# First attention: query and key parts placed by DMA through DRAM, one head to a half of the array's rows

## What is computed

```python
qkv = layernorm(x) @ w_qkv + b_qkv              # x: (16, 512, 256)
q, k, v = split into 16 heads of 16 columns
scores = einsum('bhqd,bhkd->bhqk', q, k) * 16 ** -0.5
# heads 0..3:  causal mask;  heads 4..15: causal and at most 64 tokens back
w = softmax(scores); ctx = w @ v
x = x + ctx @ w_out + b_out
```

## Time and profile before

| what | value |
|---|---|
| median of three runs | 3148.2 us (3143.63 to 3151.32) |
| span of the profiled execution, its own time | 3151.3 us, which is the slowest run (3151.32) |
| attention A within it | from the start to 1048.8 us, where SP issues the next phase's first load |
| share of the span busy: PE, DVE, ACT, POOL | 90%, 70%, 48%, 45% |

### The profile page before, as it was taken

One profiled execution on the slowest core, in us unless ns is written; L12 is line 12 of the kernel. 1 busy time (PEld: TensorE's weight loads), 2 busy tenths in 40 slices (PEclk: granted clock), 3 DMA queues, 4 the chain that ended last, 5 costly groups with the idle time before them and its releaser, 6 DMA issues. The chain is left out here.

```text
span 3151.3 us, 59461 instructions
## 1 busy us (share of the span) xinstructions
PE 2820.9 (90%) x17856; PEld 2175.0 (69%) x17856; DVE 2193.1 (70%) x5372; ACT 1499.6 (48%) x3002; POOL 1419.0 (45%) x1606
## 2 busy tenths in 40 slices
PE   6999999998999688898997999999999949999993
PEld 4565655565655457787896787778787739888872
DVE  8887787778886487765565676867777655566664
ACT  3455444454455234555775443344343317666651
POOL 1332233323333173446632533457575535655556
PEclk9999999999999788999998999999999979999996
DMA  4121111211211355657984222334343248888885
GB/s 151 48 89 49 49 55 70 68 49 56 73 58 49 134 190 178 220 195 268 324 291 145 86 76 71 99 112 127 111 127 105 96 156 300 289 304 302 299 277 155
DMA packets 208998, 465.15 MB, mean 148 GB/s; under 512 B 28448, under 2 KB 119712, under 8 KB 207648
## 3 DMA queue, kind: packets, MB, share of 16 engines
q1 hardware_dynamic: 159520, 326.86, 30.3%
q0 software_dynamic: 49152, 134.28, 12.8%
HBM read 217.24 MB, written 243.27 MB: 146 GB/s over the span
## 5 line engine op out<-in xcount | busy, mean ns | idle before, releaser
L381 POOL TENSOR_SCALAR_AFFINE_SELECT a_pt<-a_pt 128x512 f32<-128x512 f32 (+1 forms) x320 | 178.0, 556 | 669.5 <-ACT a_pt L481 668.8
L481 ACT ACTIVATE a_pt<-a_S 128x384 f32<-128x384 f32 (+3 forms) x640 | 254.6, 452 | 265.3 <-PE a_S L779 261.9
L1059 POOL DMA_INDIRECT slots<-f_xn,k_picks x256 | 260.0, 1016 | 254.2 <-PE f_Z L1567 99.7
L1842 POOL DMA_INDIRECT k_yg<-made,k_picks x224 | 223.6, 998 | 254.2 <-PE b_Y L2355 138.1
L2637 POOL DMA_INDIRECT f_yg<-made,k_picks x256 | 255.1, 997 | 170.8 <-PE f_Z L2830 89.7
L629 DVE TENSOR_REDUCE a_mx<-a_FB 128x2 f32<-128x384 f32 (+4 forms) x512 | 276.1, 591 | 26.7 <-PE a_FB L754 13.7
L751 PE MATMUL a_FB<-a_kb,a_qb 128*128 128x192 bf16 (+4 forms) x1024 | 206.1, 267 | 58.7 <-DVE a_mx L629 51.3
L1856 POOL DMA_INDIRECT slots<-b_staged,k_picks x160 | 162.3, 1015 | 105.9 <-issue 38.9
L792 PE MATMUL a_PV<-a_pt,a_vv 128*32 128x192 f32 (+4 forms) x2048 | 198.4, 371 | 2.7 <-POOL a_pt L388 2.6
L751 PEld LDWEIGHTS a_FB<-a_kb,a_qb 128*128 128x128 bf16 x1024 | 102.1, 100 | 135.1 <-DVE a_mx L629 87.0
L779 PE MATMUL a_S<-a_qs,a_ks 97*128 97x384 f32 (+3 forms) x640 | 178.3, 361 | 15.6 <-issue 15.3
(11 more groups left out here) (418 smaller groups left out, 7509.2 us busy)
## 6 DMA issues: line engine op xcount, KB each, us to landing
f_xg<-slots SPq DMA_DIRECT2D x164, 512.0 KB, 6.1
made<-f_ye SPq DMA_DIRECT2D x164, 512.0 KB, 4.0
slots<-a_zeros SPq DMA_DIRECT2D x16, 2560.0 KB, 9.2
a_xin<-in_x SPq DMA_DIRECT2D x16, 512.0 KB, 10.1
x_after_a<-a_xres SPq DMA_DIRECT2D x16, 512.0 KB, 2.9
f_wexp<-in_w_exp SPq DMA_DIRECT2D x8, 1024.0 KB, 13.4
k_xin<-bases SPq DMA_DIRECT2D x16, 512.0 KB, 5.7
x_after_b<-b_xres SPq DMA_DIRECT2D x16, 512.0 KB, 3.1
```

The lines of the kernel that those rows point to most:

```text
L381: ins = nc.gpsimd.affine_select(out=v[:, :, 0:P], in_=v[:, :, 0:P], compare_op=ALU.is_ge, fill=0.0, base=0, pattern=[[0, nh], [1, P]], cha ...
L481: nc.scalar.activation(pt[:, u % 4, b * w:(b + 1) * w], S[:, s_bank[2 * u + b], 0:w], ACT.Exp).then_inc(e_done, 1)
L1059: nc.gpsimd.indirect_dma_start(out=slots[GROUP1[s]][:, :], out_offset=bass.IndirectOffsetOnAxis(ap=picks[:, i:i + 1], axis=0), in_=xn[:, s ...
L1842: nc.gpsimd.indirect_dma_start(out=yg[:, b, k, :], out_offset=None, in_=made[GROUP1[s]][:, :], in_offset=bass.IndirectOffsetOnAxis(ap=rout ...
```

## The change

- The placement matmuls (`rk`, `rq`), their selection matrices and their copies on ACT and DVE are gone. SP instead stores the four parts of each tile of eight heads to DRAM (`store_parts`: 4 DMAs of 128 partitions x 2 KB) and loads them back (`load_parts`: 12 DMAs of 16 partitions x 4 head pairs x 2 KB) so that the even head of a pair has its 3 x 16 rows at partition 0 and the odd head at partition 64. `qs` has one column block for each pair and no zeroed rows.
- A score matmul is now of one head: 49 rows (48 of parts and one of ones) in one half of the array's rows, the even and the odd heads writing different PSUM banks. The local units have 4 matmuls of 192 columns in place of 2 of 384. The factor 1/4 moves into the exponential.
- The masked bfloat16 copies are gone. DVE makes one copy of q and one of k for each tile (`halve`); SP stores them (`store_half`) and loads each head's 16 rows to partitions 0 to 15 of `qb16` and `kb16` (`load_half`), whose other rows POOL zeroes once at the start. The rough score matmuls keep their 128 rows.
- `m_rows` issues one DMA of 2 KB for each head: 16 in place of 2.
- Slots move: k of tile 0 from 6 to 5, v from 10 and 8 to 8 and 9, the maxima one slot later, the last transposes from 23 to 24.

```diff
-    for p, slot in enumerate((15, 15, 16, 16, 18, 18, 21, 22)):
-        timed += [(slot, ("rk", p)), (slot, ("rq", p))]
+    timed = ([(4, ("T", 0)), (4, ("T", 1)), (5, ("q", 0)), (5, ("k", 0)), (6, ("q", 1)), (6, ("k", 1)),
+              (8, ("v", 0)), (9, ("v", 1))] +
+             spread(10, 6.0, MAXG) + [(16, ("mT", 0))] + spread(14, 10.0, MAXL) + [(24, ("mT", 1))])
...
+                    if core:
+                        load_parts(s, 1)
                     if not isinstance(s, int) or 2 <= s + 2 < nseq:
                         load(s + 2, par)
                     if core:
                         m_rows(s, 1)
+                    if front:
+                        store_half(s + 1, 0)
+                        store_parts(s + 1, 0)
+                        store_half(s + 1, 1)
+                        load_half(s + 1, 0)
+                        store_parts(s + 1, 1)
+                        load_half(s + 1, 1)
                     if tail:
                         at_least(sp, t_dve, summed)
                         sp.dma_start(rows, xres[:, 1 - par]).then_inc(x_stored, 16)
                         at_least(sp, x_stored, stored)
                     if front:
+                        load_parts(s + 1, 0)
                         m_rows(s + 1, 0)
                         clear(s + 1)
...
+                def load_parts(s, t):
+                    sp.wait_ge(parts_stored[t], 64 * (s + 1))
+                    if s:
+                        sp.wait_ge(s_done, ev(s - 1, 2 * NU, 2 * t_last[2 * t + 1] + 1))
...
+                    for c, dst, parts in (("k", ks, (0, 0, 1)), ("q", qs, (0, 1, 0))):
+                        for n, i in enumerate(parts):
+                            for j in range(2):
+                                r = HALF * j + n * DH
+                                sp.dma_start(dst[r:r + DH, PT * t:PT * (t + 1), :].bitcast(F32),
+                                             hilo_d[c][s % 2, i, t * P:(t + 1) * P].rearrange("(a j d) n -> j d a n", j=2, d=DH)[j]
+                                             ).then_inc(parts_loaded[t], 16)
...
+                nc.gpsimd.memset(qb16[:], 0.0).then_inc(w_ready, 1)
+                nc.gpsimd.memset(kb16[:], 0.0).then_inc(w_ready, 1)
...
-                        ins = pe.matmul(S[:, s_bank[i], 0:nh * n], ks[0:ONES + 1, h // 2, kb * P:(kb + 1) * P],
-                                        qs[0:ONES + 1, h:h + nh, kb * P:kb * P + n], start=True, stop=True)
-                        ins.then_inc(s_done, 1)
+                    for h in heads:
+                        b, c = h % 2, (h - heads[0]) // 2
+                        r = slice(HALF * b, HALF * b + ONES + 1)
+                        ins = pe.matmul(S[:, s_bank[2 * u + b], c * n:(c + 1) * n], ks[r, h // 2, kb * P:(kb + 1) * P],
+                                        qs[r, h // 2, kb * P:kb * P + n], start=True, stop=True)
```

More of the change, by code:

```diff
@@ L101 @@
 PAIRS = HEADS // 2
-ONES = 3 * PAIR
+HALF = P // 2
+ONES = 3 * DH
 BAND = P + WINDOW
@@ L177, in phase_a @@
     s_bank, s_before = rotation(2 * NU, 3)
-    by_act = [kind == "rk" or (kind == "rq" and k in BY_ACT) for kind, k in FRONT]
-    act_no = [sum(by_act[:i]) for i in range(NF)]
-    dve_no = [i - act_no[i] for i in range(NF)]
-    NFA, NFD = sum(by_act), NF - sum(by_act)
     at = {use: i for i, use in enumerate(FRONT)}
     slot_front = {u: [i for i in range(NF) if timed[i][0] == u] for u in range(2 * NU)}
-    assert timed[-1][0] - NU < timed[0][0]
+    assert timed[-1][0] - NU <= timed[0][0]
     HIGH = [("T", 0), ("T", 1)] + [(c, t) for t in range(QT) for c in ("q", "k")]
@@ L242, in phase_a @@
         zeros = sb("zeros", [P, 4 * H])
+        hilo_d = {c: nc.dram_tensor("a_%s_parts" % c, (2, 2, H, SEQ), F32, kind="Internal").ap() for c in "qk"}
+        half_d = {c: nc.dram_tensor("a_%s_half" % c, (2, H, SEQ), BF16, kind="Internal").ap() for c in "qk"}
         S = ctx.enter_context(nc.psum_tensor("a_S", [P, 3, 512], F32))
@@ L293, in phase_a @@
         mt_at = [FRONT.index(("mT", g)) for g in range(2)]
+        m_of = [max(i for i in range(NF) if FRONT[i][0] == "m" and FRONT[i][1][0][-1] // HT == t) for t in range(QT)]
         with nc.Block() as block:
@@ new lines, in load_half @@
+                def load_half(s, t):
+                    sp.wait_ge(half_stored[t], 32 * (s + 1))
+                    if s:
+                        sp.wait_ge(f_done, ev(s - 1, NF, m_of[t]))
+                    else:
+                        sp.wait_ge(w_ready, NREADY)
+                    for c, dst in (("q", qb16), ("k", kb16)):
+                        sp.dma_start(dst[0:DH, HT * t:HT * (t + 1), :],
+                                     half_d[c][s % 2, t * P:(t + 1) * P].rearrange("(h d) n -> d h n", d=DH)
+                                     ).then_inc(half_loaded[t], 16)
@@ new lines, in store_parts @@
+                def store_parts(s, t):
+                    sp.wait_ge(f_dve, ev(s, NF, at["k", t]))
+                    if s >= 2:
+                        sp.wait_ge(parts_loaded[t], 16 * PARTS * (s - 1))
+                    for c, hi, lo in (("k", kh, kl), ("q", qh, ql)):
+                        for i, src in enumerate((hi, lo)):
+                            sp.dma_start(hilo_d[c][s % 2, i, t * P:(t + 1) * P], src[:, t].bitcast(F32)
+                                         ).then_inc(parts_stored[t], 16)
@@ L443, in front_use @@
                     kind, k = FRONT[i]
-                    if kind in ("T", "q", "k", "rk", "rq") and not (kind == "rq" and not by_act[i]):
+                    if kind in ("T", "q", "k"):
                         at_least(act, f_done, ev(s, NF, i))
@@ L528, in body @@
                             tail_use(s - 1, i)
-                        if u not in ACT_FIRST:
-                            fronts()
+                        fronts()
                 nc.scalar.preload_act_table_set("natural_log_exp_and_others")
@@ L788, in context @@
                         at_least(pe, pv_out, ev(s, 4, t - 1) if t else ev(s - 1, 4, 3))
-                    at_least(pe, f_dve, ev(s, NFD, dve_no[at["v", 1]]))
-                    for j, h in enumerate(heads):
+                    at_least(pe, f_dve, ev(s, NF, at["v", 1]))
+                    for j, h in enumerate(sorted(heads, key=lambda h: (h % 2, h))):
                         r = VW * (h % 4)
```

172 lines of the change are left out of this document (57 added, 115 removed).

## The result

The changed kernel takes 3239.1 us in the median (3234.7 to 3241.5), the kernel before, run beside it, 3146.0: a ratio of 1.030, interval 1.028 to 1.032. It is 93 us slower, where 3053 us and a gain were forecast.

What follows compares the result with a forecast made beforehand. PE bounds the kernel before; after the change the DMA queue was to set the pace at 55.2 us a body over PE's 51.7. 15 x (62.6 - 55.2) = 111; 3148.2 - 111 + 16 = 3053 us, range 2965 to 3150.

Steps and rivals of the forecast that it cites:

- path of 51.7 us: PE's time per body of attention A: 62.6 - 8.6 - 4.3 + 1 = 50.7, plus 1 us waiting for copies.
- The loop's turn: Pause of all engines every second body, 3.47 us, marked "issue"; taken as contained in the 62.6 us and unchanged.
- SP's queue: SP's 59 in-order issues a body, about 33 us: not the limit, but delaying the copies, +1 us on PE.
- The PE term: PE per body: placement matmuls -8.6, wait and low clock in slots 8 to 11 -4.3, scores +1, giving 50.7 us.
- waits for maxima: Slots 8 to 11: with the masked copies gone, 2.9 us of PE idle and 1.4 us of clock go.
- The knot of VectorE: Slots 8 to 11: PE waits for a maximum behind four masked copies on DVE, some 4 us; expected to go.
- my middle value: Score matmuls per body: +1 us taken, between -4.0 with halves side by side and +7.2 without.
- Rival 3: Halves of the array don't work as such and mode changes cost the upper price: PE 57.9 us a body, 3093; chance 0.10.
- The queue's rate: Loads into 16 partitions taken at 110 GB/s, bounds 41.5 and 332: 33.4 us, so the body is 55.2 us.
- Rival 2: DMA queue overfull, each body waiting at slots 0 and 8: 3245 us at 80 GB/s, 3880 at 41.5; chance 0.16.
- Rival 1: DMA queue has room, over 123 GB/s into 16 partitions, so PE sets the pace: 2992 us; chance 0.29.
- Once only: Start and ends of attention A: first scores +3, body 0 some 15 us late behind the clears, body 15 -2; sum +16.

Runs made afterwards that it cites:

- e6: Changed kernel with the residual of the next sequence in slot 16 instead of 9 and the loop written out: 3036.6 us, ratio 0.967.
- e3: Kernel before with its loop over pairs of sequences written out: 3115.3 us, ratio 0.991.
- e10: Changed kernel, loop written out, residual in slot 16, zeros ahead of local maxima rows, 32-bit fills, maxima rows in 4 DMAs a sequence: 2991.8 us, 0.950.
- e1: Changed kernel with one number changed, GpSimd's residual of the next sequence in slot 16 instead of slot 9: 3122.0 us, ratio 0.993.
- e9: Changed kernel, loop kept, residual in slot 16, part loads of heads 8 to 15 held until slot 0's scores, zeros ahead of local maxima rows: 3061.0 us.
- e16: Kernel before with its loop written out and its zeros moved ahead of the rows of the local maxima: 3115.4 us, ratio 0.991.

## Why the prediction was wrong

Two steps failed, each a wait that the path of 51.7 us did not have.

**"The loop's turn ... contained in the 62.6, and stays" is the first.** The row said "issue", and the DMA engines were at a share of 0.03 there. I took the pause for a constant, and did not see that the part loads come to stand where it happens and push the zeros into it. It cost 61 us in the profiled runs; taking the turns out gave 87, since some 20 were there before.

**SP's queue: the delay was costed for one customer only, and this is the larger of the two.** I had SP's 59 issues, their times and the order, and counted what they do to the bf16 halves (+1 us a body; measured 1.1 in e6). The result's store, the next thing in that order, I priced as a gap in the queue. I did not ask who waits for it: the residual on GpSimd, behind it the selects, behind them TensorE. That is 6.8 us fourteen times, 95.7 us, and cancels the gain; moving the residual gave 117.

**The PE term was nearly right in its sum of work, wrong in its parts.** With both causes gone, e6's bodies are 53.7 us where the prediction's path gave 51.7 from 62.6, which includes 1 us of turns; without them, 50.7 from 61.6. Time from each instruction's start to the next's less idle, the last three bodies of e3 and of e6, divided by three:

```
us per body          e3      e6    difference   predicted
placement matmuls    8.4     0        -8.4        -8.6
scores               9.5     7.6      -1.9        +1  (-4.0 to +7.2)
rough scores        12.1    13.0      +0.9         0
all other work      27.7    28.5      +0.8         0
waits for maxima     3.9     2.9      -1.0        -2.9 and -1.4 of clock
wait for halves      0       1.1      +1.1        +1
other waits          0       0.6      +0.6         0
sum                 61.6    53.7      -7.9       -10.9
```

The knot of VectorE is the mis-sized term: freed of ten us of masked copies, TensorE still waits 2.9 us for maxima, now at the transposes of the last of them (L749) and in the rough scores. The scores came out cheaper than my middle value, without the halves working side by side: four matmuls of 192 columns take 0.40 us to the next start where two of 384 took 0.45 to 0.53, and two of 512 take 0.43 where they took 0.63. Rival 3 is out. What made the rough scores 0.9 us dearer stays open.

**The queue's rate was taken too low, and it didn't matter.** The part loads in the kernel after, joined in the last 1.5 us by the input load:

```profile
619.00:627.00 8.00, 5.64 (x38) 3.17 (x37) 4.10 (x11) 2.85 (x8) 0.81 (x2) 1.00 1.08 144
```

144 GB/s, where I took 110 and 41.5 to 332 as bounds. Then the body's queue needs 21.8 + 3.67 / 0.144 = 47.3 us, under TensorE's 53.7; e10 runs at 52. Rival 1's mechanism, the queue with room, is how the transfers behave. That its 2992 us is what e10 takes is in good part chance: e10 has the repairs, has lost the turns that the rival left in (some 20 us), and starts body 0 sooner. The Trainium skill's 104 GB/s for partitions 0 to 15 (SBUF — State Buffer, Door 1: The DMA port swizzle) was nearer to my 110 than to this; the loads in flight together here went to several groups of 16 partitions, which may be the difference, and no run tells.

**Rival 2 gave 3245 us, next to the measured 3239, for another reason.** Its mechanism was a full queue. The DMA share between 500 and 600 us is 0.63, and in e1 bodies without a turn became 7 us shorter with not a byte less. The slower side deserved its own mechanisms: a wait behind SP's order, and the turn.

**Once only:** start and body 0 together were to cost 3 + 15 us less the 7.4 of the gain, 10.6, and they cost 20.2. The first scores came 6.2 us late for 3 (61.49 for 55.27), by a cause that I hadn't, VectorE held by the fills; "some 5 us late" doesn't follow from its rows either, by which the fills end 2.9 us behind 18.55 (5.23 + 1.80 + 14.4 = 21.4). From the first scores to the second maxima it was +13.9 for +7.6, since the gain stayed out. The zeros ahead of body 0's loads were sized about right: with them elsewhere (e9 against e1) it is 13.4 us shorter, for the 15 predicted. (By the rate of the Trainium skill, the prediction's sum should read 3082, not 3083.)

**What the change is worth** is seen in e16 against e10: 124 us less. In their profiles the first start is 7.0 us later (48.7 for 41.7), body 0 is 8.7 us shorter, and the 14 bodies behind it 8.3 us each. The forecast had 111 us in the bodies, but e10 also has repairs that it didn't reckon with. So the gain was there, and the kernel as changed gave it back in waits that have nothing to do with the arithmetic.

## What to carry to other kernels

- A transfer put first on an in-order queue delays all behind it: follow each of those through its waiters, engine by engine, to the one that sets the pace, and not only the transfers one has added. Moving the waiter (slot 9 to slot 16) can be the whole repair.
- Where a loop turns, look at what the DMA engines do at that moment. A pause with "issue" as its cause is not a constant: keep the turn quiet, or write the loop out.
- A new fill of a tile at the start, on GpSimd, is not free because GpSimd is idle: VectorE can be held until it ends. Filling the same bytes as 32-bit numbers halved it.

## What the runs showed of the hardware

- A turn of the loop stops TensorE for 3.1 us with quiet DMA engines, and for 11.9 in the mean with full ones; traffic counts as far as it lies over the stop (2.5 MB more: +2.5 us of stop, +3.4 of body). The first 16 KB of instructions start within 0.5 us with quiet engines and after 2.9 to 3.4 us with full ones.
- GpSimd's fill of 8192 bf16 columns takes 6.92 us, of the same bytes as 4096 32-bit columns 3.50; a VectorE TENSOR_SCALAR of 0.17 us took 12.60 us through two of them, while TENSOR_TENSOR beside the first took its usual time.
- Two matmuls of 49 rows in the two halves of the array's rows run one behind the other, 0.43 us for 1024 columns; with 192 columns each, halves in turn or one half first makes no difference (339 and 344 ns in the mean).
- Loads of 128 KB into 16 partitions each, several in flight, reach 144 GB/s at a DMA share of 1.08.
- Twelve single-row DMAs take SP 7.5 to 8.8 us to issue; two DMAs with the same rows 1.5.
